# Three batches of a cross-attention context loaded a second time as columns, and a table of slots with gathered rows in a mixture of experts

## What is computed

```python
# 1: cross attention, 16 heads of 32
xn = layer_norm(layernorm(x), g1, b1)
cn = layer_norm(context, g2, b2)          # per context row: (c - mean) / sqrt(var + eps), then g2, b2
q, k, v = xn @ Wq.T, cn @ Wk.T, cn @ Wv.T
x = x + softmax(q k^T / sqrt(32) + mask) v @ Wo.T + bo
# 2: self attention with rotary embedding, 16 heads of 32
x = x + attention(layernorm(x)) @ Wo.T + bo
# 3: mixture of 8 experts, top 2, no capacity limit; F = 1024
rn = layernorm(layernorm(x)) * gamma + beta        # for the gate
rw, sel = top_k(softmax(rn @ gate_w.T), 2)
h = gelu(einsum(layernorm(x), w1)); y = einsum(h, w2)   # per expert
x = x + sum over the two chosen experts of rw * y
```

## Time and profile before

| what | value |
|---|---|
| median of 3 launches | 1031.93 us (1031.4 to 1032.46) |
| profiled launch, its own time | 1033.27 us |
| its span, first to last instruction | 1031.5 us |
| PE busy | 913.2 us, 89% of the span |
| DVE, ACT, POOL busy | 686.1, 527.9, 407.2 us |
| set-up, up to the first `mt` | 0 to 90 us |
| cross attention, 16 windows | 90 to 695 us |
| self attention | 695 to 809 us |
| mixture | 809 to 1031.5 us |
| DMA read, written | 95.0 MB, 11.3 MB |

### The profile page before, as it was taken

The page is one execution under the profiler, slowest core; times in us unless marked ns, Lnnn a source line. Parts: engine busy times, 40 slices in busy tenths (PEclk is TensorE's granted clock), DMA queues, the critical chain, the costliest instruction groups (busy, mean ns, idle before and its releaser), DMA issues. The chain is left out here.

```text
span 1031.5 us, 24517 instructions
## 1 busy us (share of the span) xinstructions
PE 913.2 (89%) x10397; PEld 611.0 (59%) x10397; DVE 686.1 (67%) x1010; ACT 527.9 (51%) x801; POOL 407.2 (39%) x293
## 2 busy tenths in 40 slices
PE   5988999999999999999999999767775495899996
PEld 3464676676676676676676676433443383676663
DVE  7854777646777645777644455775667495799983
ACT  3543445555345545345544345531554562899893
POOL 2020665355665355665345545422230074111112
PEclk9998999999999999999999999669997597999999
DMA  9361122443022332022332022007600355999993
GB/s 340 103 180 42 33 61 60 126 105 89 22 59 63 124 105 54 20 56 63 124 106 53 22 54 62 2 1 263 270 2 1 129 212 171 414 400 398 400 391 45
DMA packets 48455, 134.63 MB, mean 131 GB/s; under 512 B 9870, under 2 KB 11790, under 8 KB 44506
## 3 DMA queue, kind: packets, MB, share of 16 engines
q1 hardware_dynamic: 45356, 126.78, 36.1%
q0 software_dynamic: 2800, 6.04, 2.9%
q10 hardware_dynamic: 192, 0.26, 0.1%
HBM read 94.99 MB, written 11.33 MB: 103 GB/s over the span
## 5 line engine op out<-in xcount | busy, mean ns | idle before, releaser
L419 POOL TENSOR_TENSOR acc_pool<-acc_pool,pT 128x1024 f32<-128x1024 f32 x92 | 216.7, 2355 | 170.2 <-ACT pT L688 168.5
L688 ACT ACTIVATE pT<-ps_s 128x1024 f32<-128x1024 f32 x128 | 130.7, 1021 | 216.7 <-PE ps_s L857 216.4
L526 DVE TENSOR_REDUCE mpart<-ps_b 128x1 f32<-128x512 f32 x256 | 174.4, 686 | 94.7 <-PE ps_b L835 93.6
L819 PE MATMUL ps_a<-wv_hi,cT_hi 128*128 128x128 f16 x1024 | 184.4, 220 | 0.4 <-ACT kbias L608 0.4
L821 PE MATMUL ps_a<-wv_hi,cT_lo 128*128 128x128 f16 x1024 | 183.3, 219 | 0.0
L820 PE MATMUL ps_a<-wv_lo,cT_hi 128*128 128x128 f16 x1024 | 183.2, 219 | 0.0
L521 DVE TENSOR_TENSOR k_lo<-k_f,k_hi 128x512 f16<-128x512 f32 x64 | 72.3, 1129 | 70.2 <-ACT k_hi L664 69.9
L835 PE MATMUL ps_b<-k_stack,q_stack 98*128 98x512 f16 x256 | 98.6, 388 | 11.9 <-DVE mpart L526 7.7
L819 PEld LDWEIGHTS ps_a<-wv_hi,cT_hi 128*128 128x128 f16 x1024 | 99.7, 97 | 12.4 <-issue 11.9
L857 PE MATMUL ps_s<-q_stack,k_stack 98*128 98x128 f16 x1024 | 100.2, 227 | 7.3 <-ACT pT L688 6.2
L820 PEld LDWEIGHTS ps_a<-wv_lo,cT_hi 128*128 128x128 f16 x1024 | 100.2, 98 | 5.0
(11 more groups left out here) (248 smaller groups left out, 1873.9 us busy)
## 6 DMA issues: line engine op xcount, KB each, us to landing
w_raw<-in_w SPq DMA_DIRECT2D x30, 2048.0 KB, 16.8
raw<-in_context SPq DMA_DIRECT2D x16, 1024.0 KB, 5.8
k_stack<-k_hi SPq DMA_DIRECT2D x252, 64.0 KB, 2.0
k_stack<-k_lo SPq DMA_DIRECT2D x128, 64.0 KB, 2.0
slots_in<-a_zeros SPq DMA_DIRECT2D x1, 3855.0 KB, 13.6
rows_in<-slots_in SPq DMA_DIRECT2D x15, 257.0 KB, 16.3
q_stack<-k_stack SPq DMA_DIRECT2D x12, 128.0 KB, 2.4
x_sb<-in_x SPq DMA_DIRECT2D x2, 512.0 KB, 4.1
```

What stands on the lines that cost most here:

```text
L419: nc.gpsimd.tensor_tensor(acc_pool[:, :], pT[:, 0, :] if p == 1 else acc_pool[:, :], pT[:, p % PT, :], ALU.add).then_inc(pool_add, 1)
L526: nc.vector.tensor_reduce(mpart[:, j, kb:kb + 1], bank_b(step)[:, :], AX.X, ALU.max).then_inc(p1_max, 1)
L688: nc.scalar.activation(pT[:, p % PT, :], ps_s[:, :], ACT.Exp, scale=SM_SCALE).then_inc(exp_done, 1)
L819: nc.tensor.matmul(to, cT_hi[:, c, keys], t.wv_hi[:, c, col], start=(c == 0), stop=False)
```

## The change

**Context.** Batch 0 stays as it was. For batches 1 to 3 the host also hands over the context transposed (`context_columns`: per quarter of the keys, channels on 128 partitions x 4, 512 keys in a row). The steps `nm` and `t` of these batches are gone, 48 of each. In their place, per quarter `n` of 512 keys: `mo` (SP stores the four tiles' means and factors to DRAM as rows, in 4-byte pieces), `ld` (SP loads the quarter as columns over the same part of `raw`, then, once POOL's subtraction of the quarter before and DVE's multiplications of the one before that are done, the row of means and the row of factors, each spread over 128 partitions), `su` (POOL subtracts the row of means from the quarter in one instruction of 128 x 2048), `mu` (DVE multiplies by the row of factors in two instructions of 128 x 1024), and `hl` (ACT copies two halves of 128 x 1024 to `cT_hi`, DVE subtracts two to form `cT_lo`). Statistics come four tiles at a time. The tables of slots at the head of the file say where each step stands.

**Mixture.** The records that are scattered shrink to 8 bytes, weight and token number. The normalised rows are stored in order in DRAM (`rows`), as soon as each batch has them. POOL waits for the eight scatters, reads the whole table of 15 x 128 records into SBUF with a DMA of its own (`table`), and gathers the rows of each tile from tile 3 on with an indirect DMA (`gather`), four tiles ahead of the scattering addition. SP no longer waits for the scatters nor reads rows; it issues weights only. The copy `second` on ACT is gone. `y_evict` moves behind `w2_high` in ACT's loop, and `y` has three buffers in place of two. `misc_in` counts five DMAs in place of six, since the token column of `a_zeros` is gone, and the 3.9 MB of zeroed slots become 15 x 128 records of 8 bytes.

The core of the diff:

```diff
-TURNING_AT = ("", "ppp", "tptptp", "tptptp", "tptptp", "tptptp", "tptp", "tt")
+MAXIMA_BESIDE_SPLITS_AT = {1: 2, 2: 3, 3: 3, 4: 3, 5: 3, 6: 2}
+STATISTICS_AT = (0, 0, 1, 1, 2, 3, 4, 5, 6, 7, 8, 8, 9, 10, 11, 11)
+MOMENTS_AT, COLUMNS_AT, SUBTRACT_AT = (2, 6, 9, 12), (3, 7, 10, 14), (5, 9, 12, 16)
+MULTIPLY_AT = (8, 9, 12, 13, 15, 16, 17, 18)
+SPLITS_AT = (18, 19, 19, 20, 21, 21, 22, 23)
...
+                if step[0] == "mo":
+                    b, n = step[1:]
+                    sp.wait_ge(pool_pow, 3 * factors_ready(b, QUAD * n))
...
+                        sp.dma_start(io.moments[k, n, :, :].rearrange("i p -> p i"), part,
+                                     allow_slow_non_contiguous=True).then_inc(moments_out, 16)
+                if step[0] == "ld":
+                    b, n = step[1:]
+                    sp.wait_ge(moments_out, 32 * (NQ * (b - 1) + n + 1))
+                    sp.dma_start(columns(n), io.context_columns[b:b + 1, n, :, :, :].rearrange("o c p k -> (o p) c k")
+                                 ).then_inc(raw_in[n], 16)
+                    quads = NQ * (b - 1) + n
+                    if quads:
+                        sp.wait_ge(subtracted, quads)
+                    if quads >= 2:
+                        sp.wait_ge(normed, NKT + NC * (quads - 1))
...
+                if step[0] == "su":
+                    b, n = step[1:]
+                    pool.wait_ge(raw_in[n], loaded(b, as_columns=True))
+                    nc.gpsimd.tensor_tensor(columns(n), columns(n), moment_rows[:, 0:1, :].broadcast_to([P, NC, KB]),
+                                            ALU.subtract).then_inc(subtracted, 1)
...
-            sp.dma_start(zeros[:, D + 1:D + 2], io.tokens[:, NB:NB + 1], allow_slow_non_contiguous=True).then_inc(misc_in, 16)
-            sp.wait_ge(misc_in, 16 * 6)
...
-            v.wait_ge(misc_in, 16 * 6)
+            v.wait_ge(misc_in, 16 * 5)
...
-            sp.wait_ge(sent, 16 * 2 * NB)
-            for k in (*range(EARLY, ROWS_AHEAD), *range(EARLY)):
-                rows_load(k)
...
+            pool.wait_ge(sent, 16 * 2 * NB)
+            pool.dma_start(table[:, :, :], io.slots.rearrange("(n p) r -> p n r", p=P)).then_inc(table_in, 16)
+            pool.wait_ge(s.rows_stored, 16 * (NB + 1))
+            pool.wait_ge(table_in, 16)
+            for k in range(EARLY, ROWS_AHEAD):
+                gather(k)
             pool.wait_ge(s.out_sem, 16 * (NB + 1))
             for k in range(TILES):
+                if k + ROWS_AHEAD < TILES:
+                    gather(k + ROWS_AHEAD)
                 pool.wait_ge(y_out, k + 1)
                 if k:
                     pool.wait_ge(y_added, 16 * k)
```

More of the change, by code:

```diff
@@ L64, in window_steps @@
     p1 = [("p1", w + 1, j, kb) for h in range(2) for j in range(HPG) for kb in (2 * h, 2 * h + 1)] if more else []
-    turning = following and g == 2
-    t = [("t", b + 1, kt) for kt in range(NKT)] if turning else []
+    maxima_at = MAXIMA_BESIDE_SPLITS_AT if following and g == 2 else MAXIMA_AT
     steps = []
@@ L109, in window_steps @@
             steps.append(("end", p))
-    assert not p1 and not t
+    assert not p1
     return steps
@@ L447, in statistics @@
+                if kt % tiles == tiles - 1:
                     v.wait_ge(stat_dve, NKT * b + kt + 1)
+                    quads = NQ * (b - 1) + kt // QUAD
+                    if b and quads >= 2:
+                        v.wait_ge(moments_out, 32 * (quads - 1))
                     nc.vector.memset(carrier[:, :], 0.0)
-                    for n in (kt - 1, kt):
-                        last = nc.vector.bn_aggr(mv[:, n % 4, :], stats[:, n % 4, :])
+                    for n in range(kt + 1 - tiles, kt + 1):
+                        last = nc.vector.bn_aggr(mv[:, n % (2 * QUAD), :], stats[:, n % (2 * QUAD), :])
@@ L629, in _ @@
                                          ACT.Copy).then_inc(tr_hi, 1)
+                elif kind == "hl":
+                    b, i = step[1:]
+                    n, two = i // 2, slice(2 * (i % 2), 2 * (i % 2) + 2)
+                    act.wait_ge(normed, NKT * b + 2 * i + 2)
+                    nc.scalar.activation(cT_hi[:, two, KB * n:KB * (n + 1)], columns(n)[:, two, :], ACT.Copy
+                                         ).then_inc(tr_hi, 2)
                 elif kind == "fold":
@@ L1029, in _ @@
                              ).then_inc(s.w2_in[e], 16)
+            for d in range(NB - 1):
+                sp.wait_ge(m_normed, 2 * d + 1)
+                sp.dma_start(io.rows[P * d:P * (d + 1), :], t.normed[:, d, :]).then_inc(s.rows_stored, 16)
         @block.gpsimd
@@ L1371, in mixture @@
         h_hi, h_lo = [[sb(f"h_{half}{u}", [P, NF, P], F16) for u in range(2)] for half in ("hi", "lo")]
-        y = [sb(f"m_y{u}", [P, D]) for u in range(2)]
-        second = sb("m_second", [P, NB, RECORD])
+        y = [sb(f"m_y{u}", [P, D]) for u in range(Y_RING)]
+        records, table = sb("m_records", [P, 2, NB, 2]), sb("m_table", [P, TILES, 2])
         stats, mv, rstd = sb("m_stats", [P, 6]), sb("m_mv", [P, 2]), sb("m_rstd", [P, 2])
```

227 lines of the change are left out of this document (130 added, 97 removed).

## The result

| | before | after |
|---|---|---|
| median | 1032.2 us | 1180.05 us (1169.63 to 1183.68, 4 runs) |
| span of the profiled launch | 1031.5 us | 1181.9 us |
| ratio, after to before | | 1.141, 95% interval 1.134 to 1.149 |
| cross attention, from the first `mt` to the last | 573.6 us | 712.9 us |
| last `mt` to the end | 367.7 us | 378.9 us |

The prediction was 1014 us, in a range of 998 to 1031, and faster. The kernel became 148 us slower. 139.3 of the 150.4 us between the spans lie in cross attention, 11.2 behind it.

A forecast was written before the change was run, and what follows sets the result against it. The prediction took PE's instructions to bound a plain window. Its terms, -32.8 + 13.8 - 2.3 + 3.7 = -17.6 us, took the span from 1031.5 to 1013.9 us, the median to 1014 us, in a range of 998 to 1031.

The forecast's parts named there:

- Part 1: Cross attention: without the transposes, the three turning windows come down to window 1's length and window 3 shortens, -32.8 us.
- Part 2, SP: Context loads and stores on SP: stores, columns and rows of a quarter fit two slots of 4.4 us, at nothing.
- rival 4: Cross attention: moment rows outlast their two slots, POOL stands on them, windows keep 45 us; about 1032 us, chance 0.07.
- Part 2, loads: Cross attention: new subtractions, multiplications and low halves fit on POOL and DVE, DVE at 33.1 of 35.14 us.
- Part 3: Cross attention: POOL's subtractions delay DVE's multiplications and the maxima behind them, 4.6 us per batch, +13.8 us.
- Part 4: Self attention: without the token column's DMA, DVE's first bias addition starts earlier, -2.3 us.
- Part 5: Mixture: PE's restart moves later by 8.6 us, against 4.9 us gained in the loop's period, +3.7 us.
- G: Mixture: POOL's time to make the descriptors of the table's DMA, taken as 5 us, between 1.06 and 15.9.
- Rival 3: Mixture: gathers between scattering additions make POOL's queue the clock, period 13.1 in place of 11.84 us; 1045 us, chance 0.11.

The follow-up runs named there:

- e3_pieces16: Changed kernel with moments stored in 256 pieces of 16 bytes per quarter, not 1024 of 4 bytes: 1067.2 us, 1.032 of the kernel before.
- e4_columns_late: Changed kernel with SP's `ld`, the subtractions and multiplications in later slots, same stores: 1182.0 us, 1.142 of the kernel before.
- e15_no_subtraction: e3_pieces16 with POOL's subtraction cut to 32 of 2048 columns: 1047.2 us, 1.018 of the kernel before.
- e2_mixture: Kernel before with only the change's table of slots and gathers in the mixture, context as before: 1055.2 us, ratio 1.019.

## Why the prediction was wrong, step by step

**Part 1** (-32.8): the instructions went as counted (465 in the turning window for 521), the time did not. The step held that PE would set the end again once its work was gone; in `e3_pieces16` the turning window is 42.1 us in place of 35.1, with DVE busy for 38.7 of it and PE waiting for DVE's maxima, and window 3, 35.1 by the prediction, is 37.0, with 1.9 us of it the wait of its `k` matmuls for the last low half.

**Part 2, SP** (at nothing): this is the step that failed, by 124 us. It took the moments' stores at the 2.2 us of `m_second<-in_tokens`. That is a load out of DRAM in 4-byte pieces; these are stores into it. The nearest row had the same size and the wrong direction, and rival 4 used it again as its evidence against. The part also asked only who waits for the store (SP, then POOL), not what the store does to all other DMA: rival 4, the right place, was priced at 1032 us and a chance of 0.07 for that reason. With the bound "as long as two slots, and nothing else moves", the upper end would have been 12 x 8.8 us higher. Moving the wait to a later slot, the natural remedy by the prediction's own reasoning, wins nothing (`e4_columns_late`).

**Part 2, loads:** the subtraction was 4.2 us by the slope, 4.55 measured, and 4.92 in `e3_pieces16`; `mu` and `hl` were put at 1.23 + 0.44 = 1.67 us and are 2.28 and 1.83 there. DVE came out at 38.7 in the turning window, not 33.1, in `e3_pieces16`. The row of the same shape, `a_prob`, was taken where POOL is idle; 1.58 us is what it costs here even with POOL's subtraction gone.

**Part 3** (+13.8): the mechanism was right, a subtraction on POOL makes DVE's operations beside it longer and the maxima late; with the stores cured it is 17.8 us by `e15_no_subtraction`. The sum with part 1, -19.0, stands against +15.2 measured: 4 of the missing 34 us are this part's, and 30 are part 1's, which came to -2.6 for -32.8.

**Part 4** (-2.3): right in the trace, 2.5 us; the time can't tell it.

**Part 5** (+3.7): wrong by 19 us alone. G was 1.28 us, not 5, but the landing 3.4 and not 2.2. The period was the wrong term: 0.49 us per tile was rightly put down to the weights and counted as a gain of 4.9, while POOL's chain of additions, at 11.73 us just as long, was taken to stay where it was. A gather on the same queue makes it longer, and it became what PE waits for. Rival 3 had this, with 13.1 us per tile against 12.9 measured. In the changed kernel the stretch behind the last `mt` cost 11.2 us, where `e2_mixture` had 20; why it differs is left open.

## What to carry to other kernels

Cost a DMA by a row of the same direction and the same size of pieces, and ask what it does to every other transfer, not only who waits for it; where no row shows it, the range must be open upwards. Add up an engine's load, but look also at what stands behind each long instruction in its order. A scratch tensor's layout is a parameter to try: pieces joined to 16 bytes, or the rows of a pair moved together, were worth 113 and 92 us here. And where POOL makes descriptors while DVE splits weights without a gap, one wait that lets POOL go first can pay for itself.
